# First attention of a fused two-layer kernel: products with V two pairs at a time in odd steps, one normalisation on ScalarE, OT evicted by VectorE

## What is computed

```python
h = jax.nn.silu(x @ W1.T + b1) @ W2.T + b2
qkv = h @ Wg.T + bg
q, k, v = jnp.split(qkv, 3, axis=-1)            # then split into HEADS = 16, HEAD_DIM = 64
dots = jnp.einsum('bhid,bhjd->bhij', q, k) * HEAD_DIM ** (-0.5)
mask = j >= i + WINDOW                          # WINDOW = 64
dots = jnp.where(mask, -jnp.inf, dots)
attn = jax.nn.softmax(dots, axis=-1)
out = jnp.einsum('bhij,bhjd->bhid', attn, v)
out = out.transpose(0, 2, 1, 3).reshape(b, n, HEADS * HEAD_DIM)
return out @ Wo.T + bo
```

## Time and profile before

| what | value |
|---|---|
| median of 3 runs | 1749.6 us (1748.31 to 1757.02) |
| profiled execution, its own time | 1733.68 us |
| span in the profile | 1731.5 us |
| TensorE busy over the span | 1370.0 us (79%) |
| VectorE, ScalarE, POOL busy | 955.7, 902.4, 872.9 us |
| first attention | to about 700 us of the span |

### The profile page before, as it was taken

One profiled execution on the slowest core, in us unless ns is written; L12 is line 12 of the kernel. 1 busy time (PEld: TensorE's weight loads), 2 busy tenths in 40 slices (PEclk: granted clock), 3 DMA queues, 4 the chain that ended last, 5 costly groups with the idle time before them and its releaser, 6 DMA issues.

```text
span 1731.5 us, 34110 instructions
## 1 busy us (share of the span) xinstructions
PE 1370.0 (79%) x8606; PEld 955.3 (55%) x8606; DVE 955.7 (55%) x3478; ACT 902.4 (52%) x2536; POOL 872.9 (50%) x1006
## 2 busy tenths in 40 slices
PE   7999999999999998268999998027667766568681
PEld 4666666666666665157888887014444443345451
DVE  1566666666666666346333333135665666557555
ACT  5776677666777776134555554004333443335454
POOL 2788888888888888515000001655454334432003
PEclk9999999999999999679999999557887888778896
DMA  9000000000000000121222221153432233333301
GB/s 358 1 11 13 14 14 12 12 12 12 12 12 12 12 12 13 57 76 55 68 69 67 67 67 58 38 69 58 63 49 50 51 50 50 48 46 47 40 2 49
DMA packets 76454, 79.00 MB, mean 46 GB/s; under 512 B 10769, under 2 KB 69650, under 8 KB 75954
## 3 DMA queue, kind: packets, MB, share of 16 engines
q1 hardware_dynamic: 55378, 49.77, 14.0%
q0 software_dynamic: 8192, 16.79, 3.5%
q10 hardware_dynamic: 12816, 11.67, 2.0%
HBM read 47.92 MB, written 29.49 MB: 45 GB/s over the span
## 4 chain that ended last, share of the span: by engine, by line
PE 28%; DMA 8%; issue 5%; SPq 4%; DVE 4%; another core or an unknown queue 3%; ACT 2%; DVEq 2%; POOL 1%; POOLq 0%; ACTq 0%
PE psum L778 8%; PE psum L786 7%; DMA qst<-mrow 3%; PE psum L811 2%; DMA wall<-mrow 2%; PE psum L822 2%; SPq L425 2%; PE psum L885 2%; DMA qkd<-parts 1%; SPq L439 1%; PE psum L901 1%; PE psum L760 1%; PE psum L844 1%; PE psum L792 1%
## 5 line engine op out<-in xcount | busy, mean ns | idle before, releaser
L501 POOL TENSOR_SCALAR P<-P,rinv 128x192 f32<-128x192 f32 (+1 forms) x512 | 427.5, 849 | 97.4 <-DVE rinv L1131 95.1
L965 ACT ACTIVATE P<-shifted,least 128x192 f32<-128x192 f32 (+1 forms) x512 | 240.1, 471 | 116.8 <-DVE least L1117 110.0
L1320 DVE TENSOR_REDUCE mx<-psum 128x2 f32<-128x512 f32 x256 | 165.2, 686 | 146.7 <-PE psum L885 91.4
L1021 ACT ACTIVATE wall<-psum 128x1024 f32<-128x1024 f32 x128 | 131.1, 1024 | 189.6 <-PE psum L811 125.4
L1117 DVE CUSTOM_DVE_ANT_0 shifted<-psum,band 128x192 f32<-128x192 f32 (+1 forms) x512 | 169.2, 385 | 57.3 <-PE psum L668 56.6
L1004 ACT ACTIVATE hid<-psum,wA 128x256 f32<-128x256 f32 x320 | 133.7, 471 | 65.2 <-PE psum L778 63.2
L778 PE MATMUL psum<-xgT,wA 128*128 128x256 f32 x640 | 156.7, 389 | 10.4 <-DVE xgT L1259 10.4
L786 PE MATMUL psum<-hid,wB 128*128 128x256 f32 x640 | 152.0, 380 | 0.4 <-ACT yTe L1008 0.4
L491 POOL DMA_INDIRECT xs<-x1c,pos x128 | 128.5, 1004 | 41.5 <-issue 28.4
L550 POOL DMA_INDIRECT yk<-ys,posc x128 | 123.3, 963 | 49.0 <-issue 34.1
L712 PEld LDWEIGHTS psum<-ident,P 128*128 128x128 f32 x1024 | 120.3, 142 | 49.0 <-issue 24.0
(11 more groups left out here) (244 smaller groups left out, 2755.1 us busy)
## 6 DMA issues: line engine op xcount, KB each, us to landing
xg<-xs SPq DMA_DIRECT2D x80, 128.0 KB, 2.0
ys<-yrow ACTq DMA_DIRECT2D x80, 128.0 KB, 1.7
wall<-in_wall SPq DMA_DIRECT2D x1, 8232.0 KB, 35.2
qkd<-parts SPq DMA_DIRECT2D x16, 384.0 KB
qst<-qkd SPq DMA_DIRECT2D x66, 64.0 KB
kst<-qkd SPq DMA_DIRECT2D x66, 64.0 KB
wall<-qkd SPq DMA_DIRECT2D x60, 64.0 KB
hT<-in_xT SPq DMA_DIRECT2D x4, 512.0 KB, 5.7
```

The lines of the kernel that those rows point to most:

```text
L501: g.tensor_scalar(x, x, rinv[:, par, n:n + 1], None, ALU.mult).then_inc(s["pn_ready"], 1)
L965: last = sc.activation(P[:, par, it, h, 0:w], shifted[:, par, it, h, 0:w], ACT.Exp, scale=-1.0, bias=least[:, par, n:n + 1], accum_out=row ...
L1021: sc.activation(pc[:, p % 4, :, :, :].rearrange("q h j n -> q (h j n)"), ST, ACT.Exp, scale=SCALE1).then_inc(s["exps1"], 1)
L1320: v.tensor_reduce(out=mx[:, :, h], in_=SB[(par + 1 + h) % 3].rearrange("q (i n) -> q i n", i=TT), axis=mybir.AxisListType.X, op=ALU.max).t ...
```

## The change

Products with V are taken out of every step. In odd steps, directly behind the scores, TensorE now computes them for the two pairs n - 3 and n - 2, into the two halves of OTB, after one wait for PTA and PTB of pair n - 2. Wo's product of pair n - 3 keeps its place; in odd steps it uses what was computed in the same step. The copy of OTB to OT moves from ScalarE to VectorE, both pairs in one copy of 512 columns, in odd steps, between the two reciprocals. The normalisation of one of the four pieces of P (second half of the rows, head 1) moves from POOL to ScalarE, which does it in the following step, behind the copy of PTB and ahead of the exponentials; the transposes of head 1 wait for it by the new semaphore `pn1_ready`.

```diff
--- before.py
+++ after.py
@@ -269,7 +269,7 @@
 
         names = """w_in xT_in0 xT_in1 xT_in2 xT_in3 wg_in rest_in x_in wall_in cst cst2 went_on hA_mm hA_act hB_mm h_ready
             qk_mm q_ev k_ev v_mm v_ev hv_ready
-            scores shifted_ready exps rinv_ready pn_ready pt_mm ptA_ev ptB_ev pv_mm ot_ev wo_mm yT_ev
+            scores shifted_ready exps rinv_ready pn_ready pn1_ready pt_mm ptA_ev ptB_ev pv_mm ot_ev wo_mm yT_ev
             m_y var_ready pow_ready x1c_ready m_x x1T_ready m_l mask_ready m_r pos_ready xsq_ready x1_kept scat exp_w top_ready
             ksq_ready rmat_ready a_done plan_ready zrow_ready plan_out plan_in pad_in
             xg_in0 xg_in1 tin_mm xgT_ready wA_ready wB_ready up_mm hid_ready dn_mm yTe_ready tout_mm yrow_ready ys_out
@@ -495,7 +495,7 @@
                         par = p % 2
                         for h in range(2):
                             need_alone(pool, "rinv_ready", 2 * pair(b, p) + (h + 1))
-                            for it in range(TT):
+                            for it in range(TT - h):
                                 n = 2 * h + it
                                 x = P[:, par, it, h, 0:(N - WINDOW if it == 0 else N)]
                                 g.tensor_scalar(x, x, rinv[:, par, n:n + 1], None, ALU.mult).then_inc(s["pn_ready"], 1)
@@ -670,24 +670,24 @@
                                 if it == TT - 1:
                                     last.then_inc(s["scores"], 1)
 
+                    if p % 2 == 1 and is_pair(b, p, -2):
+                        need(pe, "ptA_ev", pair(b, p, -1))
+                        need(pe, "ptB_ev", pair(b, p, -1))
+                        need(pe, "ot_ev", pair(b, p, -3))
+                        bb = b - 1 if p < 2 else b
+                        for k in range(2):
+                            r = (p - 3 + k) % 8
+                            need(pe, "v_ev", 4 * bb + (2 if r < 4 else 4))
+                            for jt, c0, keys in ((0, 0, slice(N, 2 * N)), (1, WINDOW, slice(WINDOW, N))):
+                                for h in range(2):
+                                    last = mm(OTB[64 * h:64 * h + 64, k * N + c0:k * N + N], V[:, jt, r * 128 + 64 * h:r * 128 + 64 * h + 64],
+                                              PT[:, k, h, keys], start=(jt == 0), stop=(jt == 1))
+                            last.then_inc(s["pv_mm"], 1)
+
                     if is_pair(b, p, 7):
                         qk(b, p, pair(b, p, 7))
                     if is_batch(b, -1):
                         after_attention(b, p)
-
-                    if is_pair(b, p, -2):
-                        r = (p - 2) % 8
-                        need(pe, "ptA_ev", pair(b, p, -1))
-                        need(pe, "ptB_ev", pair(b, p, -1))
-                        need(pe, "ot_ev", pair(b, p, -2))
-
-                        bb = b - 1 if p < 2 else b
-                        need(pe, "v_ev", 4 * bb + (2 if r < 4 else 4))
-                        for h in range(2):
-                            mm(OTB[64 * h:64 * h + 64, 0:N], V[:, 0, r * 128 + 64 * h:r * 128 + 64 * h + 64], PT[:, par, h, N:2 * N], start=True, stop=False)
-                        for h in range(2):
-                            last = mm(OTB[64 * h:64 * h + 64, WINDOW:N], V[:, 1, r * 128 + 64 * h:r * 128 + 64 * h + 64], PT[:, par, h, WINDOW:N], start=False, stop=True)
-                        last.then_inc(s["pv_mm"], 1)
 
                     if is_pair(b, p, -3):
                         r = (p - 3) % 8
@@ -704,7 +704,9 @@
 
                     if is_pair(b, p, -1):
                         for h, bk, ev in ((0, PTA, "ptA_ev"), (1, PTB, "ptB_ev")):
-                            need(pe, "pn_ready", 4 * pair(b, p) - 2 * (1 - h))
+                            need(pe, "pn_ready", 3 * pair(b, p) - (1 - h))
+                            if h == 1:
+                                need(pe, "pn1_ready", pair(b, p))
                             need(pe, ev, pair(b, p, -1))
                             for jt in range(TT):
                                 for it in range(TT):
@@ -952,6 +954,10 @@
                         need(act, "pt_mm", 2 * pair(b, p, -1))
                         need(act, "pv_mm", pair(b, p, -3))
                         sc.activation(PT[:, par, 1, WINDOW:2 * N], PTB[:, WINDOW:2 * N], ACT.Copy).then_inc(s["ptB_ev"], 1)
+                    if is_pair(b, p, -1):
+                        need(act, "rinv_ready", 2 * pair(b, p))
+                        x = P[:, par1, 1, 1, :]
+                        sc.activation(x, x, ACT.Identity, scale=rinv[:, par1, 3:4]).then_inc(s["pn1_ready"], 1)
                     if p == 5 and is_batch(b, -1):
                         need(act, "m_x", b)
                         sc.activation(x1T[:, :], M[:, 0:N], ACT.Copy).then_inc(s["x1T_ready"], 1)
@@ -971,10 +977,6 @@
                         for it in range(TT):
                             sc.activation(sqj[:, :], x1c[:, it, :], ACT.Square, accum_out=xsq[:, it:it + 1]).then_inc(s["xsq_ready"], 1)
                             need(act, "xsq_ready", 2 * b - 1 + it)
-                    if is_pair(b, p, -2):
-                        need(act, "pv_mm", pair(b, p, -1))
-                        need(act, "wo_mm", pair(b, p, -3))
-                        sc.activation(OT[:, par, :], OTB[:, 0:N], ACT.Copy).then_inc(s["ot_ev"], 1)
                     if p == 2 and is_batch(b, -1):
 
                         need(act, "wo_mm", 8 * b)
@@ -1136,6 +1138,10 @@
                         v.tensor_scalar(ntop[:, :], top[:, :, 0], -1.0, None, ALU.mult).then_inc(s["top_ready"], 1)
                         v.drain()
                         v.tensor_copy(topif[:, :, :], topi[:, :, :])
+                    if p % 2 == 1 and is_pair(b, p, -2):
+                        need(dve, "pv_mm", pair(b, p, -1))
+                        need(dve, "wo_mm", pair(b, p, -3))
+                        v.tensor_copy(OT[:, :, :].rearrange("q k n -> q (k n)"), OTB[:, :]).then_inc(s["ot_ev"], 2)
                     if p == 7 and is_batch(b, -1):
                         need(dve, "m_r", b)
                         v.tensor_tensor(rank[:, :, :], M[:, 0:2 * E].rearrange("q (i e) -> q i e", i=TT), count[:, :].rearrange("q (o e) -> q o e", o=1).to_broadcast([128, TT, E]), ALU.add)
```

## The result

The changed kernel takes 1779.3 us (median of 4 runs, 1775.3 to 1782.1) against 1753.3 for the kernel before (4 runs, 1748.3 to 1758.7). The ratio is 1.0146, with a 95% interval of 1.0102 to 1.019: slower, as forecast, but by 26 us and not by 85, and outside the range that was given, whose lower end was 1790.

The account below looks back on a forecast made before the run. TensorE's queue was taken to bound the first attention. Steps 4 and 5 +3.1, 6 and 7 +1.05, 0 to 3 -0.3 gave +3.9 us per batch, +56 in all; clock +29; +85 on 1749.6: 1835 us, range 1790 to 1884.

Parts of the forecast that it names:

- the saving: TensorE in the first attention: three changes of tile shape of eight go, saving 0.6 us per two steps.
- The mechanism: In odd steps both pairs' products wait for VectorE's PT copy; in step 5 everything up to Wo queues behind.
- the signs that were given: TensorE pauses expected: step 5, 2 to 3.5 us before products and about 2.5 before Wo; near 1 in steps 1, 7.
- Term for steps 4 and 5, +3.1 us: Waits for PTA (3.2 us) and before Wo (2.5 us) lengthen steps 4 and 5 from 11.50 to 14.63 us.
- Steps 6 and 7, +1.05: Step 7 waits 0.8 us or more for PTA; steps 6 and 7 take 10.88 us against 9.83.
- Steps 0 to 3, -0.3: Despite a wait of 1.1 us in step 1, steps 0 to 3 take 20.69 us against 20.99.
- the sum: First attention without clock: +3.9 us per batch, +58 over fifteen batches, less the first batch's saving: +56 us.
- The clock, +29: Step 5's pauses lower TensorE's clock: one to two spells per batch at 1.3 us, fifteen batches, +29 us.
- Rival (a): The waits in the first attention come but the clock holds: 1806 us; chance 0.19.
- (b): Faster, 1702 us: VectorE's chain in steps 4 and 5 shrinks, waits stay under 3.9 us per batch; chance 0.08.
- (c): ScalarE's normalisation is not covered, delaying exponentials and copy of OT 0.46 us per odd step: 1864 us; chance 0.08.

Follow-up runs that it names:

- the normalisation alone: Kernel before with only the normalisation of the second half of the rows of head 1 moved to ScalarE: 1713.2 us, ratio 0.9825; measured again 1723.0 us, 0.9876.
- the filled kernel: Changed kernel with eight products of 256 columns, later overwritten, put ahead of step 5's wait for PTA: 1778.7 us, ratio 1.0194.

## Why the prediction was right in kind and wrong in size

- **What bounds the stage, and the saving.** TensorE's queue sets the time where nothing waits: the 3.32 us even step and the 1.66 us for two pairs came as priced. Steps 2 and 3, in which TensorE waits for nothing, went from 9.94 to 9.45 us: 0.49 saved for three changes of shape, where 0.6 was forecast. A plain step of before is 4.43 us and not 4.46, and the direct change from 64x128 to 128x64 costs up to 0.06 more than the others (1.02 against 0.96, which also holds what is left of a wait); that is the difference.
- **The mechanism.** Right, and shown by moving one block: with step 5's products behind the x1c transposes the kernel falls from 1779 to 1732 us; with one pair per step in 4 and 5 only, and everything else as changed, to 1718. The pauses stand where they were said, in front of L683 for VectorE's PT and in front of L697 for OT, and POOL no longer stands before the transposes. They are shorter than the signs that were given, 1.70 us and not 2 to 3.5 in step 5, 0.48 and 0.68 and not near 1 in steps 1 and 7.
- **Term for steps 4 and 5, +3.1 us: the first step that failed.** Both sides were sized from one batch of before. The new pair of steps was put at 14.63 us and measured 13.16: the refinement up to PTA took 2.30 us, not 3.29, the second reciprocal ended 3.79 us into step 4, not 4.15, and from the x1c transposes to the reciprocal it was 1.75, not 1.85. The old pair of steps was put at 11.50, which is the longer of its two forms: in the profile of the earlier trace rows five of the fourteen full batches took 10.5 and one 9.4, a mean of 11.0. So the new side was 1.5 us too long and the old one 0.5, the errors cancelled in part, which is luck, and the term is +2.1 and not +3.1. What failed is the 3.29 us for VectorE's chain, taken as a fixed price. Why the chain is short in the changed kernel is only in part known: wherever POOL's power had not just released it, it took 2.30 us or less, in every batch of the changed kernel and of the normalisation alone; where POOL's power had, it took 3.3 us in 8 of 13 batches of one profile of before and in 11 of 13 of the other, and 2.24 in the rest. So the release goes with the longer form and does not decide it; what does stays open.
- **Steps 6 and 7, +1.05:** 10.94 against 10.88 forecast. **Steps 0 to 3, -0.3:** 340.91 to 361.00 in the changed kernel, 20.09 against 20.69 forecast, so -0.9; the wait in step 1 is 0.48 us and not 1.1. Together a batch is 44.19 us, not 46.2; against a mean of 41.9 before that is +2.3, and not +3.9. Without spells the stage is 32 us longer (690 against 658, taking the two low spells of the filled kernel off its 693.2), where the sum had 56.
- **The clock, +29: the second.** One spell adds 1.46 us to a batch and two 3.26 (45.65 and 47.45 against 44.19), close to the 1.3 taken. But in the changed kernel they come in six and in three of the fourteen full batches and not one to two in each, so with those of the last batch the stage has some 15 and 9 us of them, and whether the medians hold them is not settled. The forecast took one low stretch behind one wait for a rule; here the same wait, 1.70 us busy of 3.40, left the clock alone in most batches. Rival (a), the waits without the clock, had 0.19 and the better size, and with its 56 us it was still 22 to 30 too long.
- **The basis.** The sum was made on a profiled execution that lies 10 to 15 us below the median of its own kernel, and both profiles of before do. The stage is 39 to 48 us longer in the profiles, the medians 26 and 34 (the 26 is against 1753.3; the runs of the kernel before that stand beside the later experiments have medians of 1745.6 to 1746.4). What is left between stage and medians, 5 us or more, stays open.
- **Rivals.** (b) would have needed the waits under 3.9 us per batch: they are 1.7 + 2.2 + 0.7 + 0.6 and 0.5 in step 1, some 5.7 in all. That is nearer to the break than the 7.75 that I counted. (c) is out: 0.50 us, covered, and worth 23 to 32 us of gain by itself. Its gain was forecast at 0.65 us per batch; it is 1.9 in a batch with the longer form, since x1c is not late any more, and 4 in the last one.

## What to carry to other kernels

When work is moved ahead of a wait or a wait ahead of work, ask what else is queued behind it in the step where the releasing engine is latest, and follow that chain to the end of the step: here the same block gained 0.5 us in steps 2 and 3 and lost 3.7 in steps 4 and 5, and choosing the step decided the sign. Measure the parts of a change alone and together: one part saved 23 to 32 us by itself and 77 beside the other, whose cost it hid in good part. And size a chain from more than one period of the profile, on both sides of the difference, since a period that looks typical may be the long one of two.

## What the runs showed of the hardware

A change of TensorE's tile shape costs 0.16 to 0.2 us: three changes less saved 0.49 us in steps 2 and 3, and of the 0.96 us of the scores 0.75 are columns by an estimate from the earlier trace rows. The same VectorE chain (three small instructions, two of 128x128 and the copy of PTA) took 3.29 us in some batches of the kernel before and 2.24 in others, in the same place of the program and released by POOL's power in both, with x1c's pair at 1.15 and 0.78 us; what decides between the two is open. With the same wait, TensorE busy 1.70 us of 3.40, the granted clock was 1.00 all through one batch and 0.52 in the next stretch in another; in which batches it falls changes from execution to execution.
